# Masking the windowed attention of layer 1: additions on TensorE before the exponential, or multiplications on GpSimd and VectorE behind it

## The chip, the cores and the metric

The kernel is one program on one core of a Trainium2 chip. The metric is device time in microseconds (us) from launch to end; lower is better. Engines are named as in the profile: PE is TensorE (PEld its weight loads), DVE is VectorE, ACT is ScalarE, POOL is GpSimd, SP is SyncE.

## What is computed

Four sequences of 1024 tokens with 128 features pass through two layers. Each layer is an attention and a mixture of experts, each with a layer norm and a residual. Layer 1's attention has two halves in a row: a global causal one and a local one with a window of 32 keys. The change touches the local one alone. Cut to what matters:

```python
def local_gqa_attn(x, wq, wk, wv, wo):          # x: (1024, 128); H = 16 heads of 8, KVH = 4, WIN = 32
    q, k, v = split_heads(x @ wq, H), split_heads(x @ wk, KVH), split_heads(x @ wv, KVH)
    q, k = qk_norm(rope(q, BASE_L)), qk_norm(rope(k, BASE_L))
    k, v = repeat_kv(k), repeat_kv(v)
    diff = i[:, None] - i[None, :]
    mask = (diff >= 0) & (diff < WIN)
    scores = jnp.where(mask, einsum('bhqd,bhkd->bhqk', q, k) / sqrt(HD), -1e30)
    return merge_heads(einsum('bhqk,bhkd->bhqd', softmax(scores), v)) @ wo
```

The heads of q and k are normed, so the scores are small and the kernel takes no maximum off them. The softmax's sum comes from a column of ones beside the values (L1481), and DVE multiplies by its inverse at the end (L1814, L1818).

## The kernel before, in words

The program runs stage after stage: attention of layer 0, mixture of layer 0, `layer1_attention`, mixture of layer 1. `layer1_attention` has eight rounds (`ROUNDS`): rounds 0 to 3 are the global attention of the four sequences, rounds 4 to 7 the local one. A round has 32 steps (`STEPS`): four groups of four heads, by eight blocks of 128 keys. Each engine has one instruction queue, written out in the order of rounds and steps, and runs it strictly in that order; semaphores join the queues.

Two steps, 2k and 2k+1, make **pair k** of a round (pairs 0 to 15). In a local round PE does a pair as `local_pair` writes it: `score` of both steps (2 matmuls each, L1633, into the two score tiles `s_ps`), `mask_scores` of both (2 matmuls each, L1645: an identity times a tile of 0 and -1e30, added onto the scores), then `weigh` of the two steps of the pair before (4 or 8 matmuls each, L1664, probabilities by values), then `fill_banks`: transposes and projections that belong to the round before, this one or the next, into the two tiles `x_ps`. The table in `shared_uses` says which goes where.

A local step covers 128 keys by at most 160 queries for four heads, so its scores and probabilities are 128 partitions by 640 numbers (512 in a group's last key block, which is always an odd step). ACT takes the exponential (L1764) of both steps of a pair, then reads the `x_ps` tiles that are its own (L1730 to L1743). In step 18 to 22 of a round it also writes the high parts of the next round's heads (L1750), for which it waits until DVE has finished `scale_heads` (L1882) of step 17. The probabilities lie in three tiles `probsT` of 1024 queries' width, step s in tile s % 3, so that ACT waits for the `weigh` of three steps ago (L1762).

DVE and POOL make the next round's inputs meanwhile. DVE in a local round: `keep_output` (L1829) at steps 0, 4, 8 and so on, the reads of turned-back outputs (L1814, L1818) and of the output projection (L1824); `square_input`, `sum_input`, `scale_input` in steps 0, 1, 2 (L1838 to L1848); `rotate` in step 13 (L1854), `square_heads` in 14 (L1857), `sum_heads` in 15 (L1861 to L1864), `inverse_roots` in 16 (ten instructions from L1869 on), `scale_heads` in 17, `fill_slots` in 19 to 23 (L1893). In rounds 5 and 6 a layer norm of the round before comes on top in steps 22 to 29: statistics, its variance in step 26 (L69), normalisation in 27 and 28 (L74), the residual in 29 (L1907). In round 7 it is the norms for the next mixture. POOL in a local round: `input_root` in step 1 (L1490, waits for `sum_input`, and `scale_input` waits for it), `rotate` in 13 (L1496), `add_rotation` in 16 (L1502, waits for `sum_heads`), and from round 5 on `inverse_root` at step 25 (L90, waits for the variance that DVE works out in step 26). In the global rounds POOL also zeroes the diagonal block of every step's probabilities (`cut_diagonal`, L1509), and PE's `weigh` waits for that; in the local rounds it does not.

Of the kernel before, what the change touches and what calls it, by code (L numbers as in the profile page):

```python
# [7 lines left out]
BF16 = mybir.dt.bfloat16  # L8
# [7 lines left out]
P = 128  # L16
# [1309 lines left out]


def last_of_half(x, c):

    return max(n for n, kb in enumerate(order_of(x)) if any(a // HALF == c for a, _ in query_cols(x, kb)))  # L1330
# [56 lines left out]
def layer1_attention(nc, g):  # L1387


    with ExitStack() as ctx:  # L1390
# [36 lines left out]
        x_filled, x_read_act, x_read_dve = sem("x_filled"), sem("x_read_act"), sem("x_read_dve")  # L1427
        scored, exp_done, cut, pv_done, o_kept = (sem(n) for n in ("scored", "exp_done", "cut", "pv_done", "o_kept"))

        heads = QK // HD  # L1430
# [35 lines left out]
        with nc.Block() as block:  # L1466
# [8 lines left out]
            def _(pool):  # L1475
# [28 lines left out]
                def cut_diagonal(r, n):  # L1504
# [5 lines left out]
                                       compare_op=ALU.is_ge, fill=0.0, base=0, channel_multiplier=-1).then_inc(cut, 1)  # L1510

                for r in range(-1, ROUNDS + 1):
                    x = r + 1
                    for n in range(STEPS):
                        if 0 <= r < BATCH:
                            cut_diagonal(r, n)
                        if x in NORM_COUNT and n == 2:
                            inverse_root(pool, norm1, g.minus_half[:, 0:NB], NORM_COUNT[x])
# [23 lines left out]
            def _(pe):  # L1542
# [74 lines left out]
                def score(r, n, unit):  # L1617
# [12 lines left out]
                    for i in range(2):  # L1630
# [3 lines left out]
                                         start=True, stop=True, skip_group_check=True)  # L1634
                    if not is_local(r):
                        last.then_inc(scored, 1)

                def mask_scores(r, n):

                    kb, u = key_block(r, n), units_before(r, n)  # L1640
                    _, at_once, a, e = units_of(r, kb)[0]
                    for i in range(2):
                        out = s_ps[u % 2][:, i * HALF:i * HALF + at_once * (e - a)]
                        keeps = g.mask_window[:, 0:e - a].unsqueeze(1).to_broadcast([P, at_once, e - a])
                        last = pe.matmul(out.rearrange("p (j n) -> p j n", j=at_once), g.ident_bf[:], keeps, start=False,  # L1645
                                         stop=True, skip_group_check=True)
                    last.then_inc(scored, 1)

                def weigh(r, n, c):
# [3 lines left out]
                    a, e = cols[c]  # L1653
                    if is_local(r) or c:
                        pe.wait_ge(exp_done, UNITS_UP_TO[r, n])
                    else:
                        pe.wait_ge(cut, steps_up_to(r, n))
# [4 lines left out]
                    for place in range(GQ):  # L1662
                        col = a - kb * P if is_local(r) else a
                        last = pe.matmul(o_ps[place * SLOT:(place + 1) * SLOT, a:e],  # L1664
                                         values[r % 2][:, kb, head_at(s, place) // GQ, :],
                                         probsT[(r * STEPS + n) % 3][:, place // 2, place % 2, col:col + e - a], start=first,
                                         stop=True, skip_group_check=True)
# [25 lines left out]
                def local_pair(r, n):  # L1693

                    score(r, n, 0)
                    score(r, n + 1, 0)
                    mask_scores(r, n)
                    mask_scores(r, n + 1)
                    late_r, late_n = (r, n - 2) if n else (r - 1, STEPS - 2)
                    if is_local(late_r):  # L1700
                        weigh_all(late_r, late_n)
                        weigh_all(late_r, late_n + 1)
                    else:
                        weigh_last_of(late_r, late_n)
                    fill_banks(r, n)
                    fill_banks(r, n + 1)
# [15 lines left out]
            def _(act):  # L1722
# [30 lines left out]
                def exponents(r, n):  # L1753
                    step, kb = r * STEPS + n, key_block(r, n)
                    for unit, (j, at_once, a, e) in enumerate(units_of(r, kb)):
                        u = units_before(r, n) + unit
                        act.wait_ge(scored, u + 1)
                        if step >= 3 and unit == 0:

                            act.wait_ge(pv_done, step - 2)  # L1760
                        col = a - kb * P if is_local(r) else a
                        out = probsT[step % 3][:, :, j:j + at_once, col:col + e - a]  # L1762
                        src = s_ps[u % 2][:].rearrange("p (k n) -> p k n", k=2)[:, :, 0:at_once * (e - a)]
# [22 lines left out]
            def _(dve):  # L1786
# [124 lines left out]
                def norm_for_mixture():  # L1911
# [30 lines left out]
                    def scale_slots():  # L1942
                        dve.wait_ge(slot_rs_ready, 1)
                        for q in range(SB):
# [5 lines left out]
                            scale_slots, *(lambda q=q: normalize(range(2 * q, 2 * q + 2)) for q in range(4))]  # L1950

                for r in range(-1, ROUNDS + 1):
                    x = r + 1
# [5 lines left out]
                    if soft_parts:  # L1959
                        assert norm_chain.n == NORMS_TO_SECOND_RESIDUAL, norm_chain.n  # L1960
                    for n in range(STEPS):
                        for kept in outputs_kept_at(r, n):
                            keep_output(*kept)
# [549 lines left out]
def build(nc, aps, out):  # L2513
    g = Shared()
    g.inputs = aps
    with ExitStack() as ctx:
# [7 lines left out]
        g.mask_kq = sb("mask_kq", [P, P], BF16)  # L2524
        g.mask_window = sb("mask_window", [P, LOCAL_W], BF16)
        first_ctx = ctx.enter_context(ExitStack())
# [3 lines left out]
        with nc.Block() as block:  # L2530
# [13 lines left out]
            def _(dve):  # L2544
                dve.wait_ge(const_loaded, 4 * 16)
                dve.tensor_copy(g.ident_bf[:], g.ident[:])
                dve.tensor_copy(g.mask_kq[:], staged[0][:, 0:P])
                dve.tensor_copy(g.mask_window[:], staged[1][:])
        attention_layer0(nc, g)
# [25 lines left out]
```

## Time and profile before

| | |
|---|---|
| median of three runs | 2423.7 us (2423.76, 2423.70, 2411.78) |
| span of the profiled execution, first to last instruction | 2408.9 us |
| its own device time | not given apart from the span; the nearest run shown is 2411.78 us, 2.9 us above the span |
| busy share of the span | PE 91%, DVE 60%, ACT 51%, POOL 44% |
| `layer1_attention`'s local rounds | about 1956 to 2167 us of the span |

A busy share is the time in which the engine had an instruction running. The profile can list groups of instructions, stretches of time, waits with what ended them, and a timeline. In a timeline row the columns are start, length, engine, line, operation, output and inputs with their shapes, how many instructions were merged, and in brackets how long the engine had been idle and what released it.

### The profile page before, as it was taken

How to read it: one execution, taken by the hardware profiler on the slowest of the kernel's cores; microseconds unless marked ns; L12 is line 12 of the kernel's file. 1: busy time of each engine (PE TensorE's matmuls, PEld its weight loads, DVE VectorE, ACT ScalarE, POOL GpSimd, SP SyncE). 2: the span in 40 equal slices, each digit the busy share in tenths (PEclk: the TensorE clock that was granted, in tenths of full speed). 3: DMA queues.
4: the chain of work that ended last, by engine and by line, in shares of the span. 5: the costliest groups of instructions: out<-in, count | busy, mean ns of one | idle time of the engine just before them, and what ended most of it. 6: DMA issues, size and time to landing. Idle time of an engine off the chain costs nothing. (4 is left out here: it accounts for less than half of the span.)

```text
span 2408.9 us, 40334 instructions
## 1 busy us (share of the span) xinstructions
PE 2199.0 (91%) x15428; PEld 1390.3 (58%) x15428; DVE 1443.0 (60%) x3248; ACT 1224.4 (51%) x1788; POOL 1048.7 (44%) x980
## 2 busy tenths in 40 slices
PE   4999999999999999994999999969999998897787
PEld 2555565555555565543888888724434455555667
DVE  3677757776677757773556565555554555656533
ACT  2555545554465545541323333267786876664533
POOL 0777757776677757773223232433333321100001
PEclk9999999999999999997999999979999999999999
DMA  2000000000000000001200000000000000003001
GB/s 76 1 1 1 1 1 1 1 1 1 1 1 1 1 1 1 1 1 35 39 1 1 1 1 1 1 1 1 1 1 1 1 1 1 2 8 71 1 1 36
DMA packets 36323, 18.19 MB, mean 8 GB/s; under 512 B 16666, under 2 KB 33956, under 8 KB 36132
## 3 DMA queue, kind: packets, MB, share of 16 engines
q1 hardware_dynamic: 36132, 15.61, 2.6%
q8 instruction: 125, 2.05, 0.4%
q14 instruction: 66, 0.54, 0.1%
HBM read 13.50 MB, written 2.10 MB: 6 GB/s over the span
## 5 line engine op out<-in xcount | busy, mean ns | idle before, releaser
L311 POOL TENSOR_TENSOR a_first<-a_first,a_ring 128x512 f32<-128x512 f32 (+3 forms) x352 | 558.8, 1588 | 141.9 <-ACT a_ring L556 106.5
L1764 ACT ACTIVATE g_probsT<-g_s_ps 128x1024 f32<-128x1024 f32 (+2 forms) x448 | 368.9, 868 | 136.6 <-PE g_s_ps L1633 83.3
L556 ACT ACTIVATE a_ring<-a_st 128x768 f32<-128x768 f32 (+1 forms) x256 | 234.6, 916 | 262.8 <-PE a_st L463 262.8
L478 PE MATMUL a_o_ps<-a_ring,a_v 128*64 128x512 f32 (+3 forms) x1280 | 249.2, 485 | 3.4 <-POOL a_ring L293 2.4
L645 DVE RECIPROCAL a_row_inv<-a_row_inv 128x512 f32<-128x512 f32 x64 | 213.8, 3342 | 16.8 <-ACT a_row_inv L544 16.8
L1034 ACT ACTIVATE m_silu<-m_up,m_b 128x512 f32<-128x512 f32 x160 | 109.6, 688 | 221.9 <-PE m_up L966 219.1
L623 DVE TENSOR_REDUCE a_part_max<-a_mx 128x2 f32<-128x1024 f32 x128 | 156.5, 1222 | 102.4 <-PE a_mx L434 99.1
L1664 PE MATMUL g_o_ps<-g_probsT,g_values 128*32 128x512 f32 (+5 forms) x2688 | 206.7, 419 | 5.5 <-POOL g_probsT L1509 5.1
L1633 PE MATMUL g_s_ps<-g_qT,g_kT 64*128 64x512 f32 (+3 forms) x896 | 172.7, 433 | 28.0 <-ACT g_probsT L1764 22.4
L1509 POOL TENSOR_SCALAR_AFFINE_SELECT g_probsT<-g_probsT 128x512 f32<-128x512 f32 x128 | 88.0, 691 | 246.1 <-ACT g_probsT L1764 246.0
L630 DVE CUSTOM_DVE_ANT_0 a_masked<-a_mx,mask_wide,a_part_max 128x256 bf16<-128x256 f32 (+3 forms) x256 | 128.3, 548 | 91.1 <-PE a_mx L434 90.6
L887 POOL TENSOR_TENSOR m_acc<-m_acc,m_part 128x512 f32<-128x512 f32 x54 | 69.8, 1292 | 221.6 <-DVE m_part L1192 221.2
L630 DVE CUSTOM_DVE_ANT_0 a_masked<-a_mx,mask_wide 128x256 bf16<-128x256 f32 (+3 forms) x256 | 112.7, 487 | 82.6 <-PE a_mx L434 82.6
L1633 PEld LDWEIGHTS g_s_ps<-g_qT,g_kT 64*128 64x128 f32 x896 | 77.1, 187 | 140.9 <-ACT g_probsT L1764 98.4
L463 PE MATMUL a_st<-a_q_hi,a_k_hi 64*128 64x512 f32 (+3 forms) x768 | 150.7, 386 | 4.0 <-ACT a_shift L534 3.1
L434 PE MATMUL a_mx<-a_k_hi,a_q_hi 64*128 64x512 f32 (+3 forms) x768 | 141.0, 388 | 12.6 <-DVE a_largest L630 11.8
L980 PEld LDWEIGHTS m_down<-m_w,m_glu 128*128 128x128 f32 x1280 | 149.6, 192 | 3.5
L980 PE MATMUL m_down<-m_w,m_glu 128*128 128x128 f32 x1280 | 149.7, 275 | 0.0
L1180 DVE SCALAR_TENSOR_TENSOR m_glu<-m_up,m_b,m_silu 128x512 f32<-128x512 f32 x160 | 115.1, 745 | 45.5 <-ACT m_silu L1034 45.5
L463 PEld LDWEIGHTS a_st<-a_q_hi,a_k_hi 64*128 64x128 f32 x768 | 73.4, 185 | 113.8 <-ACT a_ring L556 79.1
L966 PE MATMUL m_up<-m_xT_hi,m_w_hi 128*128 128x512 f32 x320 | 134.1, 419 | 1.8 <-DVE m_xT_lo L1132 1.4
L463 PE MATMUL a_st<-a_q_hi,a_k_lo 64*128 64x512 f32 (+3 forms) x768 | 135.3, 344 | 0.0
(310 smaller groups left out, 4372.8 us busy)
## 6 DMA issues: line engine op xcount, KB each, us to landing
m_w<-in_L_ffn_rw SPq DMA_DIRECT2D x2, 1024.0 KB, 8.3
s_w<-in_L_ffn_w SPq DMA_DIRECT2D x1, 2048.0 KB, 9.0
s_w<-in_L_ffn_w SPq DMA_DIRECT2D x4, 512.0 KB, 10.2
out_x<-x SPq DMA_DIRECT2D x8, 256.0 KB, 2.3
m_w<-in_L_ffn_rw SPq DMA_DIRECT2D x2, 512.0 KB, 5.1
x<-in_L_attn_x SPq DMA_DIRECT2D x1, 512.0 KB, 4.5
a_outT<-in_L_attn_w_q SPq DMA_DIRECT2D x1, 512.0 KB, 5.4
a_outT<-in_L_attn_w_k SPq DMA_DIRECT2D x1, 512.0 KB, 6.0
```

The costliest lines, as they stand in the source:

```text
L311: pool.tensor_tensor(total[:, h, q:q + w], total[:, h, q:q + w], probs_of(n, u)[:, h, off:off + w], ALU.add).then_inc(added, 1)
L434: last = pe.matmul(mx_ps[:, h, off:off + w], q_hi[m % 2][rows_of(h), i * P:(i + 1) * P], k_hi[m % 2][rows_of(h), key:key + w], start=True, ...
L463: last = pe.matmul(out[:, h, off:off + w], a[rows_of(h)], r[rows_of(h)], start=i == 0, stop=i == len(todo) - 1)
L478: last = pe.matmul(o_ps[rows_of(h), first_q:first_q + w], v_half[n // 4 % 2][:, j, head:head + A_HD], probs_of(n, u)[:, h, off:off + w], s ...
L556: act.activation(probs_of(n, u)[:, :, 0:w], st_ps[u % 2][:, :, 0:w], ACT.Exp).then_inc(exp_done, 1)
L623: last = dve.tensor_reduce(part_max[:, i, :], mx_ps[:], AX.X, ALU.max)
L630: last = dve.tensor_tensor_reduce(masked[1 - part][:, h, 0:w], mx_ps[:, h, off:off + w], g.mask_wide[:, HALF - w:HALF], 1.0, so_far, ALU.a ...
L645: dve.reciprocal(row_inv[c][:], row_inv[c][:]).then_inc(inv_ready, 1)
L980: last = pe.matmul(down[u % 2][:, t * P:(t + 1) * P], glu[u % 2][h][:, t * P:(t + 1) * P], w3[:, e, h, :], start=h == 0 and t == 0, stop=h ...
L1633: last = pe.matmul(out, kT[r % 2][s // 2][rows, kb * P:(kb + 1) * P], qT[r % 2][rows, j:j + at_once, a:e], start=True, stop=True, skip_gro ...
L1664: last = pe.matmul(o_ps[place * SLOT:(place + 1) * SLOT, a:e], values[r % 2][:, kb, head_at(s, place) // GQ, :], probsT[(r * STEPS + n) % ...
L1764: act.activation(out, src.rearrange("p k (j n) -> p k j n", j=at_once), ACT.Exp, scale=float(HD) ** -0.5).then_inc(exp_done, 1)
```

## The change

The local rounds lose `mask_scores`. The tile of 0 and -1e30 (`mask_window`) becomes a tile of ones and zeros in bf16 (`mask_keep`), and `cut_window` multiplies each local step's probabilities by it, in place, after the exponential. POOL does it for even steps, at the head of the step in its queue, and counts `cut`. DVE does it for odd steps, at the head of the step in its queue, and counts `cut_odd`. PE's `weigh` waits for these counts where it waited for `exp_done`. `probs_place` gives the local rounds six places for probabilities: each of the three tiles is used in two halves (columns 0 to 159 and 256 to 415), so that ACT waits for the `weigh` of six steps ago.

```diff
+def probs_place(r, n):
+    step = r * STEPS + n
+    return step % 3, step % 6 // 3 * 256 if is_local(r) else 0
...
@@ gpsimd
+                def cut_window(r, n):
+                    w = units_of(r, key_block(r, n))[0][3] - key_block(r, n) * P
+                    buf, at = probs_place(r, n)
+                    probs = probsT[buf][:, :, :, at:at + w]
+                    keeps = g.mask_keep[:, 0:w].unsqueeze(1).unsqueeze(1).to_broadcast([P, 2, 2, w])
+                    pool.wait_ge(exp_done, UNITS_UP_TO[r, n])
+                    pool.tensor_tensor(probs, probs, keeps, ALU.mult).then_inc(cut, 1)
...
                         if 0 <= r < BATCH:
                             cut_diagonal(r, n)
+                        if BATCH <= r < ROUNDS and n % 2 == 0:
+                            cut_window(r, n)
                         if x in NORM_COUNT and n == 2:
...
@@ tensor
-                    if not is_local(r):
-                        last.then_inc(scored, 1)
-
-                def mask_scores(r, n):
-                    kb, u = key_block(r, n), units_before(r, n)
-                    _, at_once, a, e = units_of(r, kb)[0]
-                    for i in range(2):
-                        out = s_ps[u % 2][:, i * HALF:i * HALF + at_once * (e - a)]
-                        keeps = g.mask_window[:, 0:e - a].unsqueeze(1).to_broadcast([P, at_once, e - a])
-                        last = pe.matmul(out.rearrange("p (j n) -> p j n", j=at_once), g.ident_bf[:], keeps, start=False,
-                                         stop=True, skip_group_check=True)
                     last.then_inc(scored, 1)
...
-                    if is_local(r) or c:
+                    if is_local(r):
+                        done = steps_up_to(r, n) - BATCH * STEPS
+                        if n % 2:
+                            pe.wait_ge(cut_odd, done // 2)
+                        else:
+                            pe.wait_ge(cut, BATCH * STEPS + (done + 1) // 2)
+                    elif c:
                         pe.wait_ge(exp_done, UNITS_UP_TO[r, n])
...
                     score(r, n, 0)
                     score(r, n + 1, 0)
-                    mask_scores(r, n)
-                    mask_scores(r, n + 1)
...
@@ scalar
-                            act.wait_ge(pv_done, step - 2)
-                        col = a - kb * P if is_local(r) else a
-                        out = probsT[step % 3][:, :, j:j + at_once, col:col + e - a]
+                            act.wait_ge(pv_done, step - 5 if step >= BATCH * STEPS + 3 else step - 2)
+                        buf, at = probs_place(r, n)
+                        col = at + a - kb * P if is_local(r) else a
+                        out = probsT[buf][:, :, j:j + at_once, col:col + e - a]
...
@@ vector: the same cut_window, with dve and .then_inc(cut_odd, 1)
                     for n in range(STEPS):
+                        if BATCH <= r < ROUNDS and n % 2:
+                            cut_window(r, n)
                         for kept in outputs_kept_at(r, n):
                             keep_output(*kept)
...
@@ build
-                dve.tensor_copy(g.mask_window[:], staged[1][:])
+                dve.tensor_scalar(g.mask_keep[:], staged[1][:], 0.0, None, ALU.is_ge)
```

## Rows read from the trace of the kernel before

**Rows 1.** The page, part 1: busy time of the engines over the span

```profile
PE 2199.0 (91%) x15428; PEld 1390.3 (58%) x15428; DVE 1443.0 (60%) x3248; ACT 1224.4 (51%) x1788; POOL 1048.7 (44%) x980
```

**Rows 2.** Busy time in stretches: the local rounds, then three parts of them

```profile
core 0: us, PE busy (x) PEld busy (x) DVE busy (x) ACT busy (x) POOL busy (x), PEclk, DMA share, GB/s
1956.00:2167.00 211.00, 186.09 (x2114) 122.05 (x2112) 121.07 (x318) 133.52 (x236) 30.13 (x18) 0.97 0.01 3
...
1996.00:2009.00 13.00, 12.93 (x128) 7.93 (x128) 4.47 (x14) 10.39 (x20) 0.00 (x0) 0.80 0.01 1
2009.00:2035.00 26.00, 24.60 (x280) 16.89 (x280) 7.62 (x15) 19.56 (x36) 1.68 (x2) 1.00 0.01 2
2035.00:2051.00 16.00, 10.97 (x131) 7.36 (x129) 15.32 (x31) 5.32 (x10) 5.71 (x3) 1.00 0.00 1
```

**Rows 3.** Groups by line and shape, 1956 to 2167 us: exponentials and mask matmuls

```profile
L1764 ACT ACTIVATE g_probsT<-g_s_ps 128x640 f32<-128x640 f32 x112 | 78.1, 704 | 50.0 <-PE g_s_ps L1645 45.6 <-PE g_o_ps L1664 1.6
L1645 PE MATMUL g_s_ps<-mask_window,ident_bf 128*128 128x320 bf16 x224 | 42.8, 309 | 0.0
```

**Rows 4.** Timeline of PE: round 5's pairs 0, 3, 4, 7, 12, round 6's 0

```profile
2012.59 0.56 PE L1633 MATMUL g_s_ps<-g_qT,g_kT 64*128 64x320 f32 x4 [0.74 <-ACT g_qT L1732]
...
2021.96 0.53 PE L1633 MATMUL g_s_ps<-g_qT,g_kT 64*128 64x320 f32 x4
...
2024.73 0.56 PE L1633 MATMUL g_s_ps<-g_qT,g_kT 64*128 64x320 f32 x4
...
2034.17 0.53 PE L1633 MATMUL g_s_ps<-g_qT,g_kT 64*128 64x320 f32 x4
...
2055.17 0.85 PE L1633 MATMUL g_s_ps<-g_qT,g_kT 64*128 64x320 f32 x4
...
2067.86 0.56 PE L1633 MATMUL g_s_ps<-g_qT,g_kT 64*128 64x320 f32 x4 [0.74 <-ACT g_qT L1732]
```

**Rows 5.** Timelines of PE and of ACT: the rest of round 5's pair 4

```profile
2025.22 0.72 PE L1645 MATMUL g_s_ps<-mask_window,ident_bf 128*128 128x320 bf16 x4
2025.87 0.70 PE L1664 MATMUL g_o_ps<-g_probsT,g_values 128*32 128x160 f32 x16
2026.49 1.09 PE L1549 MATMUL g_x_ps<-ident,g_att 128*128 128x128 f32 x8
2027.52 0.56 PE L1633 MATMUL g_s_ps<-g_qT,g_kT 64*128 64x320 f32 x4
...
2025.70 1.48 ACT L1764 ACTIVATE g_probsT<-g_s_ps 128x640 f32<-128x640 f32 x2 [0.22 <-PE g_s_ps L1645]
2027.19 1.08 ACT L1738 ACTIVATE g_attT<-g_x_ps 128x512 f32<-128x512 f32 x2
```

**Rows 6.** Timeline, round 5's pairs 7 to 11: VectorE, GpSimd and PE's next scores

```profile
2034.93 0.82 DVE L1854 TENSOR_TENSOR g_part<-g_qk,g_cos 128x640 f32<-128x640 f32 x1 [1.43 <-ACT g_values L1743]
2034.97 1.92 POOL L1496 TENSOR_TENSOR g_part<-g_qk,g_sin 128x640 f32<-128x640 f32 x1 [15.46 <-ACT g_values L1743]
...
2035.67 1.90 DVE L1854 TENSOR_TENSOR g_part<-g_qk,g_sin 128x640 f32<-128x640 f32 x1
...
2036.85 1.85 POOL L1496 TENSOR_TENSOR g_part<-g_qk,g_cos 128x640 f32<-128x640 f32 x1
...
2038.04 2.00 DVE L1857 TENSOR_TENSOR g_turned<-g_qk 128x1280 f32<-128x1280 f32 x1
...
2048.28 1.48 DVE L1882 TENSOR_TENSOR g_turned<-g_turned,g_rs 128x1280 f32<-128x1280 f32 x1
...
2051.77 0.41 PE L1633 MATMUL g_s_ps<-g_qT,g_kT 64*128 64x320 f32 x2 [2.70 <-ACT g_probsT L1764]
```

**Rows 7.** GpSimd's multiplications and additions: a group, and one in a global round

```profile
L311 POOL TENSOR_TENSOR a_first<-a_first,a_ring 128x512 f32<-128x512 f32 x128 | 165.2, 1291 | 16.1 <-POOL a_ring L293 15.4 <-POOL a_first L311 0.5 <-ACT a_ring L556 0.2
...
1731.81 1.27 POOL L1496 TENSOR_TENSOR g_part<-g_qk,g_sin 128x640 f32<-128x640 f32 x1
```

**Rows 8.** Timeline, round 5's pairs 1 and 2: GpSimd's root, VectorE behind it

```profile
2017.86 1.65 POOL L1490 TENSOR_TENSOR g_rs_h<-g_ss_h,minus_half 128x8 f32<-128x8 f32 x1 [29.20 <-DVE g_ss_h L1844]
...
2019.54 1.23 DVE L1848 TENSOR_TENSOR normed<-hidden,g_rs_h 128x1024 f32<-128x1024 f32 x1 [1.00 <-POOL g_rs_h L1490]
```

**Rows 9.** Timeline, round 5's pairs 13 and 14: PE, and the norm's root

```profile
2061.09 0.91 PE L1633 MATMUL g_s_ps<-g_qT,g_kT 64*128 64x320 f32 x4
...
2062.22 1.65 POOL L90 TENSOR_TENSOR norm_rstd<-norm_var,minus_half 128x8 f32<-128x8 f32 x1 [17.78 <-DVE norm_var L69]
```

More of the change, by code:

```diff
@@ L1428, in layer1_attention @@
         scored, exp_done, cut, pv_done, o_kept = (sem(n) for n in ("scored", "exp_done", "cut", "pv_done", "o_kept"))
+        cut_odd = sem("cut_odd")
         heads = QK // HD
@@ L1662, in weigh @@
                     for place in range(GQ):
-                        col = a - kb * P if is_local(r) else a
+                        buf, at = probs_place(r, n)
+                        col = at + a - kb * P if is_local(r) else a
                         last = pe.matmul(o_ps[place * SLOT:(place + 1) * SLOT, a:e],
                                          values[r % 2][:, kb, head_at(s, place) // GQ, :],
-                                         probsT[(r * STEPS + n) % 3][:, place // 2, place % 2, col:col + e - a], start=first,
+                                         probsT[buf][:, place // 2, place % 2, col:col + e - a], start=first,
                                          stop=True, skip_group_check=True)
@@ L1758, in exponents @@
                         if step >= 3 and unit == 0:
-                            act.wait_ge(pv_done, step - 2)
-                        col = a - kb * P if is_local(r) else a
-                        out = probsT[step % 3][:, :, j:j + at_once, col:col + e - a]
+                            act.wait_ge(pv_done, step - 5 if step >= BATCH * STEPS + 3 else step - 2)
+                        buf, at = probs_place(r, n)
+                        col = at + a - kb * P if is_local(r) else a
+                        out = probsT[buf][:, :, j:j + at_once, col:col + e - a]
                         src = s_ps[u % 2][:].rearrange("p (k n) -> p k n", k=2)[:, :, 0:at_once * (e - a)]
@@ L1950, in norm_for_mixture, with cut_window @@
                             scale_slots, *(lambda q=q: normalize(range(2 * q, 2 * q + 2)) for q in range(4))]
+                def cut_window(r, n):
+                    w = units_of(r, key_block(r, n))[0][3] - key_block(r, n) * P
+                    buf, at = probs_place(r, n)
+                    probs = probsT[buf][:, :, :, at:at + w]
+                    keeps = g.mask_keep[:, 0:w].unsqueeze(1).unsqueeze(1).to_broadcast([P, 2, 2, w])
+                    dve.wait_ge(exp_done, UNITS_UP_TO[r, n])
+                    dve.tensor_tensor(probs, probs, keeps, ALU.mult).then_inc(cut_odd, 1)
                 for r in range(-1, ROUNDS + 1):
@@ L2524, in build @@
         g.mask_kq = sb("mask_kq", [P, P], BF16)
-        g.mask_window = sb("mask_window", [P, LOCAL_W], BF16)
+        g.mask_keep = sb("mask_keep", [P, LOCAL_W], BF16)
         first_ctx = ctx.enter_context(ExitStack())
```

## The prediction, made before the change was run

> **What bounds the kernel now.** I began with the page: PE is busy for 91% of the span [rows 1], so one would expect matmuls taken away to be time won. But the change lives in the local rounds alone, 211 us, so I read that stretch. There PE is busy for 186.1, ACT for 133.5, DVE for 121.1 and POOL for 30.1 us [rows 2]. These shares average over two regimes. From 2009 to 2035 us PE is busy for 24.6 of 26 us: PE sets the pace. From 2035 to 2051 DVE is busy for 15.3 of 16 us and PE for only 11.0: DVE's queue sets it [rows 2].
>
> I cut round 5 by the starts of its pairs [rows 4]: A, pairs 0 to 2, 9.37 us; B, pairs 3 to 6, 12.21; C, pairs 7 to 11, 21.00; D, pairs 12 to 15, 12.69; together 55.27. Rounds 4 and 6 repeat it within a microsecond, except that round 4 has no layer norm in D. Round 7 has no next round's heads to make.
>
> Pair 4 is the clean PE-bound one: scores at 2024.73, masks at 2025.22, `weigh` at 2025.87, fill at 2026.49, next pair at 2027.52. The masks take 0.65 of its 2.79 us. ACT works 1.48 + 1.08 us of them [rows 4, 5].
>
> **What goes.** 256 mask matmuls, of which the 224 wide ones are 42.8 us busy [rows 3]. On PE's path it is 0.65 us a pair, 41.6 us over 64 pairs if PE bounded all. It doesn't. In pairs 3 and 4 ACT then needs 1.45 + 1.08 = 2.53 us a pair, so 0.26 is won, not 0.65. In the projection pairs 5 and 6 PE's fill is longer, and 0.5 each is won. B: 2 x 0.26 + 2 x 0.5 = **1.6 us won a round**.
>
> **What comes.** 64 multiplications of 128x640 on POOL and 64 on DVE (48 of 640, 16 of 512). On DVE one costs 0.82, about 0.75 back to back, by L1854 [rows 6]. On POOL the same size, also with a broadcast operand, took 1.27 when undisturbed, and 512 dense elements took 1.29, so 640 would take at most 1.61 [rows 7]. The new one is dense like the second and broadcast like the first; I take 1.4. What the bf16 operand does no row shows; I put it at nothing. [...]
>
> **They shut each other out.** In rows 6 DVE's first product runs 2034.93 to 2035.75 and POOL's, begun at 2034.97, ends at 2036.89: 0.82 of waiting and 1.13 of work. DVE's second ends at 2037.57, 0.68 after that; POOL's second at 2038.70, 1.13 after that; DVE's L1857 at 2040.04, 1.34 after that. They take strict turns. So I charge a turn wherever a POOL cut meets a DVE instruction with two inputs in SBUF. The skill's page SBUF — State Buffer, section "Who interferes with whom", states it as an exclusive lock for the whole instruction, which speaks against giving the two halves of this mask to these two engines; the trace agrees. Were there no such turns, the sum below would be about +3 us instead of +21.
>
> **The order of the queues.** `weigh` of a step waited for ACT; now it waits for a cut standing in POOL's or DVE's queue behind all that these do for other rounds. Before, DVE could lag by more than a pair without PE noticing.
>
> A. POOL's cut 0 (1.4) blocks DVE's `square_input` for about 0.7, and cut 1 (0.75) stands before `sum_input`. POOL's root then ends at 2019.51 in the old times [rows 8], cut 2 comes after it (2020.9) and blocks `scale_input` (1.15, to 2022.05); then cut 3 (0.8), the read of a bank (0.6) and the second half of pair 2's fill (0.55): pair 3 at about 2024.0 + 1.4 instead of 2021.96, 3.5 late. Less 0.65 and some slack won in pairs 0 and 1: **+2.5**.
>
> C. DVE's chain from `rotate` to `scale_heads` runs 2034.93 to 2049.76, 14.8 us without a gap, and pair 11 waits for it through ACT: 2.70 us idle [rows 6]. Into it go cuts 15 and 17 (2 x 0.75), POOL's cut 14, which gets its turn after L1857 and before cut 15 (1.4), and POOL's cut 18 among `inverse_roots` (1.3 to 1.4): 4.2 to 4.3. PE stands meanwhile in pair 8 for cut 14, and in pair 9 some 8 us for cut 17, queued behind `inverse_roots`; that it then does pair 10 late adds little. **+4.4**.
>
> D. In rounds 5 and 6 the norm's root ends at 2063.87 [rows 9]. It stands in POOL's queue before cut 26, which so ends at 2065.3, while `weigh` of step 26 would be due at 2061.09 + 0.5: up to 3.7 late. Cuts 25, 27 and 29 lengthen DVE's queue beside the norm (4 x 0.75 in D). Less about 1 won: **+2.5**. In round 4 there is no norm: ACT-bound, **-1.9**.
>
> Round 7 has no chain C, but two roots (steps 3, 7) and the norm's at 25 before a cut: about +2, +1, +2.5; its other pairs win 3: **+2.5**.
>
> Free: two more waits on PE, the wider choice of places (ACT waited only 1.6 us for `weigh` in the wide group, [rows 3]), one constant made by another operation. No DMA moves, and SP's queue isn't touched.
>
> **Sum.** 3 x 2.5 - 3 x 1.6 + 3 x 4.4 - 1.9 + 2 x 2.5 + 2.5 = +21.5 us on the profiled span of 2408.9. The median of the runs is 14.8 above that span; I add the sum to the median: **2445 us**, +0.9%. Measurement of this kernel can tell about 0.5%, 12 us, from no change.
>
> **Rivals.**
> - *The order costs little.* POOL and DVE take turns less often, or the waits overlap more than by my hand count. The no-turns case, +3 us: 2427. For it: DVE has half of the stretch free. Against: the 15.3 of 16 us. Chance 0.25.
> - *PE's saving comes through.* DVE would have to have each odd cut done one pair later, at most some 3.3 us after the scores. Then half the pairs win 0.26 and half 0.6: 64 x 0.43 = 27 us, 2397. For it: 24.6 of 26 us PE-bound, POOL busy for only 30 of 211. Against: chain C. Chance 0.12. This is the case on the other side; it decides wherever DVE has under about 0.8 us of other work per pair, as in B.
> - *The clock falls.* After PE's first long wait the granted clock is 0.80 over 13 us [rows 2], partly the 1.2 GHz level; there PE is busy for 12.93 of 13. With waits of 5 and 8 us in C, and more in A and D, PE could come back at that level each time. If some 10 us of full-clock work a round at twice its time come in the open in part, 6 us a round: about +40, 2464. Chance 0.13.
> - That it doesn't do what it says I hold for unlikely: the cut products have their own semaphore, and nothing else reads uncut places.
>
> **How the numbers follow.** Main case +21 (chance 0.5; own range +10 to +33). Range 2414 to 2466: below it lies nearly all of the second rival, above it the tail of the third. A tenth of the main case lies within 12 us of no change, and the first rival all of it: same 0.25 + 0.05 = 0.30, slower 0.45 + 0.13 = 0.58, faster 0.12.
>
> **What would show it.** No L1645 rows. POOL rows of 1.3 to 1.5 us, longer when DVE is at a two-input product, and 128 more DVE and POOL rows. PE idle before L1664 with POOL and DVE as releasers, 20 us a round or more; in pair 9 one wait of about 8 us. Pairs 3 to 6 of a round in about 10.6 us; `rotate` to `scale_heads` in 19 us instead of 14.8. Wrong would be: local rounds shorter than 211 us; cuts on DVE that never wait for POOL; or a POOL cut above 2 us, which would make POOL the bound.

## The result, and the profile of the changed kernel

The changed kernel takes **2463.93 us** (median of four runs, 2462.47 to 2467.45), the kernel before 2419.75 (four runs, 2411.78 to 2423.76): a ratio of 1.0194, with an interval of 1.0165 to 1.0223. I had forecast 2445, slower. The direction is right and the time lies in the range, but the loss is 44.2 us where my sum said 21.5. The kernel before ran 54 times more beside the experiments, with medians of 2415.94, 2416.48 and 2415.98 us; against these the loss is 48 us.

The page, part 1, answers to [rows 1]:

```profile
PE 2193.7 (89%) x15172; PEld 1390.3 (57%) x15172; DVE 1536.0 (62%) x3312; ACT 1216.7 (49%) x1788; POOL 1151.6 (47%) x1044
```

256 matmuls are gone and PE is busy for only 5.3 us less. DVE has 93.0 us more, POOL 102.9 more.

The start of the local rounds wanders by some 15 us from one execution to the next, with the same code ahead of it, so I compare their length, from the first local score to the end of the last output projection, in the one profiled execution of each kernel. Where kernels have the same code in a section this length repeats well: section C of round 5 (pairs 7 to 11) takes 21.00 us in the kernel before and 21.01 and 21.02 in two kernels further down that leave it alone. Busy time in stretches, the kernel before (a stretch not shown above, with its last round):

```profile
1955.00:2171.40 216.40, 190.47 (x2144) 125.53 (x2144) 123.14 (x325) 135.40 (x239) 30.38 (x18) 0.97 0.01 3
...
2123.00:2171.40 48.40, 44.80 (x536) 29.46 (x536) 27.00 (x99) 26.54 (x40) 4.28 (x3) 1.00 0.04 10
```

The same for the changed kernel, then its round 5 in C and in D, and its round 7:

```profile
1952.20:2221.70 269.50, 186.30 (x1888) 124.06 (x1888) 215.36 (x389) 126.89 (x239) 133.41 (x82) 0.78 0.01 3
...
2044.59:2068.87 24.28, 14.57 (x142) 9.76 (x141) 23.20 (x41) 9.29 (x23) 13.65 (x9) 0.72 0.00 1
2068.87:2089.08 20.21, 13.33 (x124) 8.87 (x120) 16.07 (x39) 10.04 (x18) 9.20 (x6) 0.66 0.00 1
...
2160.00:2221.70 61.70, 43.76 (x472) 27.83 (x472) 49.84 (x114) 24.68 (x40) 28.74 (x19) 0.78 0.02 5
```

The whole loss is here: 269.5 - 216.4 = **53.1 us**, beside 51.8 between the two profiled spans (2460.7 and 2408.9). PE has 256 of 2144 matmuls fewer and is busy for nearly as long as before, with a granted clock of 0.78 where it was 0.97: partly the 1.2 GHz level. It is idle for 83.2 us instead of 25.9. DVE is busy for 80% of the stretch, before for 57%, and in C for 23.2 of 24.3 us. In C it sets the pace; elsewhere PE waits in turn for its cuts and for POOL's.

The waits of the local rounds (engine, what waited, who released it: us in total, times, longest) say how PE feels it:

```profile
PE g_o_ps L1678 <- DVE g_probsT L1972: 41.5, 28, 4.4
PE g_o_ps L1678 <- POOL g_probsT L1526: 38.6, 22, 4.4
```

80.1 of PE's 83.2 idle us stand before `weigh` (L1678), half of them put down to each engine's cuts. In the kernel before, PE's only wait there was this one:

```profile
PE g_o_ps L1664 <- ACT g_probsT L1764: 0.4, 1, 0.4
```

Groups of instructions by line and shape, and one tile (lowest, median and longest ns), in the same stretch:

```profile
L1972 DVE TENSOR_TENSOR g_probsT<-g_probsT,mask_keep 128x640 f32<-128x640 f32 x48 | 50.8, 1057 | 2.6 <-ACT g_probsT L1777 2.5
L1972 DVE TENSOR_TENSOR g_probsT<-g_probsT,mask_keep 128x512 f32<-128x512 f32 x16 | 21.4, 1337 | 8.1 <-ACT g_probsT L1777 8.1
L74 DVE TENSOR_SCALAR hidden<-hidden,norm_mean,norm_rstd 128x128 f32<-128x128 f32 x24 | 14.3, 655 | 2.9 <-POOL norm_rstd L90 2.9
...
L1526 POOL TENSOR_TENSOR g_probsT<-g_probsT,mask_keep x64: 1388/1407/2678, 1953.6 to 2210.5; 128x640 f32<-128x640 f32 x64
```

POOL's cut costs 1.41 us by its median, as taken (1.4). DVE's costs 1.06 and 1.34 by its means, and the smaller shape, a group's last key block, costs *more*: a mean that runs against the size is a sign that the instruction waits inside its own record. In this stretch 13 of the 16 smaller ones run beside a cut of POOL's and take 1.49 us on average, the other three 0.68. And an instruction with which the change has nothing to do, the norm's L74, takes 655 ns. Before it took 341 (and the integer `tensor_scalar` of `inverse_roots`, needed further down, 410):

```profile
L74 DVE TENSOR_SCALAR hidden<-hidden,norm_mean,norm_rstd 128x128 f32<-128x128 f32 x24 | 6.7, 341 | 3.6 <-POOL norm_rstd L90 3.6
...
L1869 DVE TENSOR_SCALAR g_rs<-g_ssq 128x160 int32<-128x160 int32 x3 | 1.2, 410 | 0.0
```

The timeline of the changed kernel's round 5, in A, C and D, answers to [rows 4, 6, 8, 9]:

```profile
2018.62 0.56 PE L1651 MATMUL g_s_ps<-g_qT,g_kT 64*128 64x320 f32 x4 [0.74 <-ACT g_qT L1744]
...
2024.50 1.65 POOL L1497 TENSOR_TENSOR g_rs_h<-g_ss_h,minus_half 128x8 f32<-128x8 f32 x1 [3.23 <-DVE g_ss_h L1857]
...
2026.12 3.73 POOL L1526 TENSOR_TENSOR g_probsT<-g_probsT,mask_keep 128x640 f32<-128x640 f32 x2
2026.18 2.41 DVE L1861 TENSOR_TENSOR normed<-hidden,g_rs_h 128x1024 f32<-128x1024 f32 x1 [1.21 <-POOL g_rs_h L1497]
...
2028.52 2.01 DVE L1972 TENSOR_TENSOR g_probsT<-g_probsT,mask_keep 128x640 f32<-128x640 f32 x1
...
2030.58 0.76 PE L1678 MATMUL g_o_ps<-g_probsT,g_values 128*32 128x128 f32 x16 [2.54 <-DVE g_probsT L1972]
...
2033.17 0.85 PE L1651 MATMUL g_s_ps<-g_qT,g_kT 64*128 64x320 f32 x4
...
2044.59 0.53 PE L1651 MATMUL g_s_ps<-g_qT,g_kT 64*128 64x320 f32 x4
...
2049.09 4.44 POOL L1526 TENSOR_TENSOR g_probsT<-g_probsT,mask_keep 128x640 f32<-128x640 f32 x2
...
2051.78 1.20 PE L1678 MATMUL g_o_ps<-g_probsT,g_values 128*32 128x160 f32 x16 [4.40 <-POOL g_probsT L1526]
...
2061.85 0.76 PE L1678 MATMUL g_o_ps<-g_probsT,g_values 128*32 128x160 f32 x8 [4.44 <-DVE g_probsT L1972]
...
2068.87 0.56 PE L1651 MATMUL g_s_ps<-g_qT,g_kT 64*128 64x320 f32 x4
...
2078.83 2.16 POOL L90 TENSOR_TENSOR norm_rstd<-norm_var,minus_half 128x8 f32<-128x8 f32 x1 [7.29 <-DVE norm_var L69]
...
2080.96 2.75 POOL L1526 TENSOR_TENSOR g_probsT<-g_probsT,mask_keep 128x640 f32<-128x640 f32 x2
2081.03 3.28 DVE L74 TENSOR_SCALAR hidden<-hidden,norm_mean,norm_rstd 128x128 f32<-128x128 f32 x4 [0.98 <-POOL norm_rstd L90]
2082.41 1.30 PE L1678 MATMUL g_o_ps<-g_probsT,g_values 128*32 128x160 f32 x24 [4.14 <-POOL g_probsT L1526]
...
2089.08 0.56 PE L1651 MATMUL g_s_ps<-g_qT,g_kT 64*128 64x320 f32 x4 [0.74 <-ACT g_qT L1744]
```

The starts of the scores cut the round as in the prediction (us):

| round 5 | A | B | C | D | sum |
|---|---|---|---|---|---|
| before | 9.37 | 12.21 | 21.00 | 12.69 | 55.27 |
| after | 14.55 | 11.42 | 24.28 | 20.21 | 70.46 |
| difference, measured | +5.2 | -0.8 | +3.3 | +7.5 | +15.2 |
| difference, forecast | +2.5 | -1.6 | +4.4 | +2.5 | +7.8 |

By rounds it is +8.8, +15.2, +15.7 and +13.3 us in rounds 4 to 7, where I had +3.4, +7.8, +7.8 and +2.5. So C is sized about right, B wins half of its gain, and what failed is A, D and round 7.

### The profile page after: what moved, and what is told of

Its sections match the earlier page's. It is cut to its first block and busy times, and to the rows that moved or that the text cites. A ratio compares the mean times of both kernels' runs of the same rounds, so it can differ in the third digit from the quotient of the medians.

```text
span 2460.7 us, 39950 instructions
## 1 busy us (share of the span) xinstructions
PE 2193.7 (89%) x15172; PEld 1390.3 (57%) x15172; DVE 1536.0 (62%) x3312; ACT 1216.7 (49%) x1788; POOL 1151.6 (47%) x1044
## 5 line engine op out<-in xcount | busy, mean ns | idle before, releaser
L1777 ACT ACTIVATE g_probsT<-g_s_ps 128x1024 f32<-128x1024 f32 (+2 forms) x448 | 362.7, 869 | 144.4 <-PE g_s_ps L1651 141.9
L1678 PE MATMUL g_o_ps<-g_probsT,g_values 128*32 128x512 f32 (+5 forms) x2688 | 222.2, 439 | 85.8 <-DVE g_probsT L1972 41.5
L1678 PEld LDWEIGHTS g_o_ps<-g_probsT,g_values 128*32 128x32 f32 x2688 | 68.1, 117 | 188.1 <-DVE g_probsT L1972 54.8
L434 PE MATMUL a_mx<-a_k_hi,a_q_hi 64*128 64x512 f32 (+3 forms) x768 | 141.1, 388 | 12.5 <-DVE a_largest L630 11.8
L1526 POOL TENSOR_TENSOR g_probsT<-g_probsT,mask_keep 128x640 f32<-128x640 f32 x64 | 101.9, 1598 | 86.7 <-ACT g_probsT L1777 86.7
```

Of the source, the lines that this page charges most:

```text
L434: last = pe.matmul(mx_ps[:, h, off:off + w], q_hi[m % 2][rows_of(h), i * P:(i + 1) * P], k_hi[m % 2][rows_of(h), key:key + w], start=True, ...
L1777: act.activation(out, src.rearrange("p k (j n) -> p k j n", j=at_once), ACT.Exp, scale=float(HD) ** -0.5).then_inc(exp_done, 1)
```

## The experiments

**Does it lie in the removal, the order or the work?** Three kernels take the change apart. The first is the changed kernel with no cut at all:

```diff
-                        if BATCH <= r < ROUNDS and n % 2 == 0:
-                            cut_window(r, n)
...
-                    if is_local(r):
...
+                    if is_local(r) or c:
                         pe.wait_ge(exp_done, UNITS_UP_TO[r, n])
```

> Leaves out the window's mask altogether (no masks on TensorE, no cuts): TensorE's weigh waits for the exponential alone, with the six places. It is the price of the removal by itself. By my prediction's sum the pairs bound by TensorE or ScalarE win 0.26 to 0.65 us each and the chain on VectorE stays: 15 to 27 us faster than before (ratio 0.989 to 0.994). If the removal itself were of no use, or harmful through the granted clock, it would be within 6 us of before.

Measured: 2397.57 us, 0.9923 of before (0.9895 to 0.9952), as expected.

The second keeps every cut, its place and its waits, but makes it 8 elements wide (on POOL and on DVE):

```diff
-                    probs = probsT[buf][:, :, :, at:at + w]
-                    keeps = g.mask_keep[:, 0:w].unsqueeze(1).unsqueeze(1).to_broadcast([P, 2, 2, w])
+                    probs = probsT[buf][:, 0, 0, at:at + 8]
+                    keeps = g.mask_keep[:, 0:8]
```

> Every cut stays where it stands in the two queues, with its waits and counts, but multiplies 8 columns of one head instead of all (so most of the mask is left out). Theory 1, the order of the queues: TensorE still waits in pairs 2, 8, 9, 14 for what stands ahead of the cuts, so most of the loss stays: slower than before by 10 to 25 us. Theory 2, the load and the turns at SBUF: with products of about 0.2 us the loss is gone, and the time is that of the kernel without cuts plus 5 us at most.

Measured: 2407.24 us, 0.9961 (0.9938 to 0.9984): between the two theories, 9.7 us above the kernel without cuts. A small cut takes 0.2 us on POOL and 0.16 on DVE, by their medians.

The third does nearly all the multiplying, on columns of the tiles that nobody uses in the local rounds, and no other engine waits for it (`weigh` waits for `exp_done`, as in the first). It has 62 products an engine instead of 64, since the first two pairs of round 4 have none, and each product also waits for the one three before it on its own engine, which is not shown:

```diff
-                    probs = probsT[buf][:, :, :, at:at + w]
+                    probs = probsT[0][:, :, :, 512:512 + w]
...
-                    pool.tensor_tensor(probs, probs, keeps, ALU.mult).then_inc(cut, 1)
+                    pool.tensor_tensor(probs, probsT[2][:, :, :, 512:512 + w], keeps, ALU.mult).then_inc(cut, 1)
...
-                    probs = probsT[buf][:, :, :, at:at + w]
+                    probs = probsT[1][:, :, :, 512:512 + w]
...
-                    dve.tensor_tensor(probs, probs, keeps, ALU.mult).then_inc(cut_odd, 1)
+                    dve.tensor_tensor(probs, probsT[2][:, :, :, 512:512 + w], keeps, ALU.mult).then_inc(cut_odd, 1)
```

> The full products stay in both queues at the same places, but read and write unused columns (512 on) of the probability tiles, and TensorE's weigh waits for the exponential alone (the mask is left out of the result). Theory 2, load and turns: near the changed kernel, at least 30 us slower than before. Theory 1, order: only VectorE's chain of pairs 7 to 11 is longer, by 4 us a round, against what the removal wins: within 12 us of before.

Measured: 2449.68 us, 1.0139 (1.0111 to 1.0167): theory 2.

Their local rounds, in this order, each row from its own kernel's stretches:

```profile
1965.00:2159.70 194.70, 157.83 (x1888) 111.89 (x1888) 122.37 (x325) 125.51 (x239) 30.37 (x18) 0.89 0.01 4
```

```profile
1967.50:2171.20 203.70, 167.47 (x1888) 115.86 (x1888) 129.98 (x389) 125.55 (x239) 50.09 (x82) 0.87 0.01 3
```

```profile
1957.20:2208.60 251.40, 175.05 (x1888) 121.65 (x1888) 217.65 (x387) 126.13 (x239) 127.00 (x80) 0.80 0.01 3
```

From 216.4 of before: the removal (with the six places) gives 21.7 us back; the order of the queues costs 203.7 - 194.7 = 9.0; the work costs 251.4 - 194.7 = **56.7**, though no other engine waits for its result. The medians of whole executions say 18.4, 9.7 and 52.1. With both one would expect 260.4; the changed kernel has 269.5, 9 us more. That remainder is a balance: by rounds it is +7.4, +5.5, +2.7 and -6.7 us, for in round 7 the work alone (65.7 us) is slower than the changed kernel (61.7). In round 5's D the work alone adds 0.6 us and the order alone 1.3 to the 12.5 of the first kernel, both together 7.8: there the late cuts and PE's wait for them feed each other.

**Whose work?** The same load with only POOL's 62 products (DVE's call taken out), then with only DVE's (POOL's taken out):

```diff
@@ vector, for POOL's alone
-                        if BATCH <= r < ROUNDS and n % 2:
-                            cut_window(r, n)
@@ gpsimd, for DVE's alone
-                        if BATCH <= r < ROUNDS and n % 2 == 0:
-                            cut_window(r, n)
```

> Of the load experiment only GpSimd's 62 products stay, on unused columns; VectorE has none and nobody waits for a cut (the mask is left out). If turns at SBUF carry the loss: 12 to 25 us above the kernel without cuts, with two-input products of VectorE drawn out to 1.4 us more. If VectorE's own products carry it: within 5 us of the kernel without cuts.

> Of the load experiment only VectorE's 62 products stay (the mask is left out). If VectorE's own time carries the loss: 30 to 50 us above the kernel without cuts, since 62 products of 0.8 us are 50 us in its queue. If turns carry it: 5 to 15 us, the products in its bound stretches alone (2 or 3 a round, 0.75 each, in three rounds).

Measured: 2428.51 us, 1.0043 (1.0025 to 1.0060), with POOL's, more than I had expected; 2407.29 us, 0.9971 (0.9958 to 0.9984), with DVE's. POOL's first:

```profile
1960.60:2188.50 227.90, 169.80 (x1888) 120.23 (x1888) 153.54 (x325) 126.02 (x239) 123.23 (x80) 0.82 0.01 3
```

```profile
1956.20:2167.60 211.40, 167.29 (x1888) 117.14 (x1888) 164.72 (x387) 125.88 (x239) 32.10 (x18) 0.84 0.02 3
```

In the first of them DVE has exactly the 325 instructions of the kernel without cuts, and is busy for 153.5 us instead of 122.4. The local rounds are 33.2 us longer, about those 31. DVE's own 62 products add 42.3 us to its queue and only 16.7 to the rounds. So a product on POOL, which had been busy for only 30 of 216 us, costs twice what it costs on DVE itself (by the medians of whole executions 30.9 us against 9.7). It isn't that POOL's roots come late behind the products: DVE's waits for POOL's results add up to 8.8 us with and without them. The timeline of POOL's load in round 7 shows how a product costs so much:

```profile
2151.12 7.94 POOL L1529 TENSOR_TENSOR g_probsT<-g_probsT,mask_keep 128x640 f32<-128x640 f32 x5
2151.18 3.43 DVE L1955 SCALAR_TENSOR_TENSOR normed<-normed,hidden 128x128 f32<-128x128 f32 x4 [0.53 <-POOL hidden L1557]
...
2154.65 3.15 DVE L1933 TENSOR_SCALAR hidden<-x,hidden 128x128 f32<-128x128 f32 x4
...
2160.65 3.42 PE L1614 MATMUL g_x_ps<-g_w_o,g_attT 128*128 128x128 f32 x16 [4.94 <-DVE g_att L1828]
```

POOL had stood in a root that waits for DVE. Five cuts had piled up behind it, and they now run back to back. Beside each of them one small DVE instruction waits for about its length, and at most one more passes before the next: four of L1955 in 3.43 us, four of L1933 in 3.15, and PE stands 4.94 us for what DVE does next. And L1933 is a `tensor_scalar`: a form that I had not counted among those that wait.

**Reads or writes?** POOL's products of the third kernel become memsets of about the same length, which read nothing:

```diff
-                    pool.tensor_tensor(probs, probsT[2][:, :, :, 512:512 + w], keeps, ALU.mult).then_inc(cut, 1)
+                    pool.memset(probsT[0][:, :, :, 512:888], 0.0).then_inc(cut, 1)
```

> The load experiment with GpSimd's products replaced by memsets of 1504 elements (about 1.4 us, the same length and places), which read nothing from SBUF; VectorE's products stay (the mask is left out). If GpSimd's reading is what shuts VectorE out: the time of the run with VectorE's products alone, within 5 us. If any work of GpSimd does: the time of the load experiment.

Measured: 2425.66 us, 1.0042 (1.0027 to 1.0057), local rounds of 227.8 us, 16.4 more than with DVE's products alone: the expectation missed. Groups by line show why:

```profile
L1529 POOL MEMSET g_probsT<- 128x1504 f32 x62 | 83.9, 1353 | 64.0 <-ACT g_probsT L1774 61.3 <-POOL g_probsT L1529 0.4
L1973 DVE TENSOR_TENSOR g_probsT<-g_probsT,mask_keep 128x640 f32<-128x640 f32 x46 | 38.0, 825 | 5.5 <-ACT g_probsT L1774 5.4
L74 DVE TENSOR_SCALAR hidden<-hidden,norm_mean,norm_rstd 128x128 f32<-128x128 f32 x24 | 15.0, 1117 | 2.9 <-POOL norm_rstd L90 2.9
L1973 DVE TENSOR_TENSOR g_probsT<-g_probsT,mask_keep 128x512 f32<-128x512 f32 x16 | 10.9, 684 | 5.7 <-ACT g_probsT L1774 5.7
L1879 DVE TENSOR_SCALAR g_rs<-g_ssq 128x160 int32<-128x160 int32 x3 | 5.0, 1683 | 0.0
...
L1955 DVE SCALAR_TENSOR_TENSOR normed<-normed,hidden 128x128 f32<-128x128 f32 x4 | 1.1, 348 | 0.1
```

Here is the same group of products with no load on POOL:

```profile
L1971 DVE TENSOR_TENSOR g_probsT<-g_probsT,mask_keep 128x640 f32<-128x640 f32 x46 | 37.6, 818 | 5.7 <-ACT g_probsT L1772 5.6
L1971 DVE TENSOR_TENSOR g_probsT<-g_probsT,mask_keep 128x512 f32<-128x512 f32 x16 | 11.0, 686 | 6.1 <-ACT g_probsT L1772 6.1
```

Beside POOL's writes a DVE product runs undisturbed (825 against 818 ns, 684 against 686), and L1955 with two inputs too (348 ns, where POOL's products made it 916). The `tensor_scalar` instructions wait all the more: L74 takes 1117 ns instead of 342. So beside POOL's reads DVE's instructions with two inputs in SBUF wait, and beside POOL's writes `tensor_scalar` does; a product does both. Not every form waits. Beside POOL's products (the run with these alone) DVE's copies out of PSUM and its reductions stay within 2 ns of the kernel without cuts (686 and 1474 ns):

```profile
L1839 DVE COPY g_outT<-g_o_ps 128x512 f32<-128x512 f32 x34 | 23.3, 686 | 39.6 <-PE g_o_ps L1675 39.6
...
L1871 DVE TENSOR_REDUCE g_ssq<-g_turned 128x160 f32<-128x1280 f32 x3 | 4.4, 1476 | 0.0
```

Of the 34 copies 19 run at the same time as one of POOL's products, and so do all three of these reductions.

**Would one engine alone do better?** All 128 cuts on DVE, then all on POOL; `weigh` waits for that engine's count alone:

```diff
@@ vector, for all on DVE (POOL's call taken out)
-                        if BATCH <= r < ROUNDS and n % 2:
+                        if BATCH <= r < ROUNDS:
                             cut_window(r, n)
@@ gpsimd, for all on POOL (DVE's call taken out)
-                        if BATCH <= r < ROUNDS and n % 2 == 0:
+                        if BATCH <= r < ROUNDS:
                             cut_window(r, n)
```

> All 128 cuts on VectorE, each at the head of its step, none on GpSimd; the mask is whole. Turns theory (VectorE's loss is mostly waiting for GpSimd's products, 44 us in the changed kernel): 128 products are about 98 us in VectorE's queue, but without turns, so faster than the changed kernel by 15 to 35 us, 2430 to 2450 us, products at 0.82 and 0.68 us in every round. Own-load theory (VectorE's products themselves are the loss): slower than the changed kernel, above 2470 us.

> All 128 cuts on GpSimd, none on VectorE; the mask is whole. Turns theory: twice as many GpSimd products of 1.4 us, 180 us and more in its queue; VectorE's other work in the local rounds is drawn out by about 60 us (31 with 62 products), and the roots stand behind more cuts: slower than the changed kernel, 2470 to 2500 us. If it were the sum of both engines' work that counts, it would be within 10 us of the changed kernel.

Measured: 2459.42 us, 1.0188 (1.0160 to 1.0216), and 2475.20, 1.0245 (1.0219 to 1.0270). All on DVE, then all on POOL:

```profile
1953.40:2210.60 257.20, 185.65 (x1888) 120.48 (x1888) 218.12 (x453) 127.06 (x239) 34.40 (x18) 0.79 0.01 3
```

```profile
1959.70:2235.40 275.70, 193.50 (x1888) 124.59 (x1888) 183.29 (x325) 126.98 (x239) 213.84 (x146) 0.77 0.01 3
```

With twice the cuts and no turns DVE is busy for 218.1 us; with half of them and the turns it was 215.4. The help of POOL is worth nothing to DVE. Taking the turns away gains 12.3 us in the profiled execution, but only 4.5 by the medians, which their intervals can't tell from nothing. Neither of the two times that I had named came (2430 to 2450, or above 2470): the queue on DVE is as full as before. With all cuts on POOL, DVE's own work is drawn out by 60.2 us (183.3 against the 123.1 of before).

**Is it the clock?** The granted clock fell as in my third rival, and its time, 2464, is the measured one. To test it, PE gets idle matmuls before `weigh` in pairs 2, 8, 9 and 14, where it would stand anyway; first in all local rounds, then in rounds 4 to 6:

```diff
+                SPINS = {2: 20, 8: 20, 9: 22, 14: 20}
...
+                            for _ in range(SPINS[n // 2]):
+                                pe.matmul(x_ps[k % 2][:, 0:480].rearrange("p (j n) -> p j n", j=3), g.ident_bf[:], keeps, start=True, stop=True, skip_group_check=True)
```

> The changed kernel, and TensorE runs 20 to 22 idle matmuls of 480 columns (about 0.2 us each at full clock, results unused) before weigh in pairs 2, 8, 9 and 14 of each local round, where it waits longest. Theory 3, the granted clock that falls after long waits carries a large part of the loss: granted clock of the local rounds above 0.9 instead of 0.78 and 15 to 25 us faster than the changed kernel. If the clock's loss lies in time that TensorE would wait anyway: within 6 us of the changed kernel; if the idle matmuls outlast the waits: slower.

> As the run with idle matmuls, but only in rounds 4 to 6, since in round 7 they stood where TensorE had no long wait. If the granted clock carries some of the loss: 5 to 10 us faster than the changed kernel (2.6 us a round was seen in rounds 5 and 6). If it carries none: within 3 us of it.

Measured: 2473.01 us, 1.0235 (1.0209 to 1.0262), and 2464.37, 1.0209 (1.0181 to 1.0237). The stretch of each:

```profile
1959.50:2233.20 273.70, 229.73 (x2196) 137.27 (x2196) 216.36 (x389) 126.02 (x239) 131.56 (x82) 0.91 0.01 3
```

```profile
1954.50:2220.90 266.40, 219.88 (x2134) 133.00 (x2134) 217.47 (x389) 126.25 (x239) 132.43 (x82) 0.89 0.01 3
```

The clock rises from 0.78 to 0.91 and 0.89, so the low clock follows from PE's waits. The first wins 2.5 and 2.7 us in rounds 5 and 6 and loses 8.9 in round 7. The second wins as much in rounds 5 and 6, loses 1.4 us in round 7, where its code is that of the changed kernel, has 3.1 us shorter local rounds in all, and the same median as the changed kernel, where I had named 5 to 10 us less if the clock carried some of the loss. Its idle matmuls:

```profile
L1716 PE MATMUL g_x_ps<-mask_keep,ident_bf 128*128 128x480 bf16 x246 | 51.9, 367 | 5.4 <-DVE g_att L1844 3.7 <-DVE hidden L1850 1.7
```

Without them PE is busy for 219.9 - 51.9 = 168.0 us, 18.3 less than in the changed kernel, yet only 3.1 us of that come through. Either it lies in time in which PE would wait for DVE and POOL anyway, or the idle matmuls, which themselves stand 5.4 us for a bank, take back part of what the clock gives; these runs cannot tell the two apart.

**A version that keeps only what wins.** By the table B is the one section that gains. The next kernel takes the masks on PE everywhere, as before, except in steps 6 to 13 of each local round, where POOL cuts the even and DVE the odd steps:

```diff
+CUT_STEPS = range(6, 14)
+is_cut = lambda n: n in CUT_STEPS
...
+                    if not is_cut(n):
+                        mask_scores(r, n)
+                        mask_scores(r, n + 1)
```

> Cuts only in steps 6 to 13 of each local round (pairs 3 to 6, where VectorE is idle), the mask matmuls everywhere else. Theory: these pairs win about 2 us a round and lose nothing elsewhere: 5 to 9 us faster than before (ratio 0.996 to 0.998). The rival, that cuts cost wherever they stand: no faster than before.

Measured: 2418.16 us, 1.0016 (1.0001 to 1.0030), no faster than before: the expectation missed. Rounds 4 to 6 won 2.6, 1.5 and 1.0 us; round 7, which has DVE work of its own there, lost 6.5. So the last kernel moves round 7's cuts to steps 14 to 23 and gives all of them, even and odd, to DVE:

```diff
+CUT_STEPS = {r: range(14, 24) if r == ROUNDS - 1 else range(6, 14) for r in range(BATCH, ROUNDS)}
...
+                        if BATCH <= r < ROUNDS and is_cut(r, n):
+                            cut_window(r, n)
```

> The mask stays on TensorE except in pairs 3 to 6 of rounds 4 to 6 and pairs 7 to 11 of round 7, where VectorE is mostly idle and cuts all steps alone. No GpSimd product, so no turns. Expected: 2 us won in each of rounds 4 to 6 and 2 to 4 us in round 7, 8 to 10 us faster than before (ratio 0.9955 to 0.997). If cuts on VectorE cost as much as masks on TensorE even there: within 4 us of before.

Measured: **2409.92 us** (twelve runs) beside 2415.98 of before, 0.9971 (0.9954 to 0.9988).

```profile
1957.60:2169.00 211.40, 183.18 (x2076) 120.96 (x2076) 147.62 (x360) 127.60 (x239) 30.39 (x18) 0.95 0.01 3
```

Its 34 cuts give 5.0 us of local rounds, 1.0, 2.1, 1.3 and 0.6 by rounds, and in round 5 B takes 10.35 us instead of 12.21. It is 6 us faster than the kernel before, where I had expected 8 to 10.

## Why the prediction was right and wrong

**Right.** The loss sits in the local rounds; POOL's cut costs 1.40 us (1.41); the two engines take turns; DVE's queue and not PE's saving decides. In C `rotate` to `scale_heads` takes 18.4 us, from 2045.35 to 2063.79, where I had 19; PE waits for cut 14 in pair 8 (4.40 us), as told. B wins, 0.8 instead of 1.6.

**The step that failed** is "They shut each other out": "So I charge a turn wherever a POOL cut meets a DVE instruction with two inputs in SBUF." I charged 0.7 + 1.15 us in A and 1.4 + 1.35 in C, 4.6 a round, 14 us in rounds 4 to 6, and nothing in B, D and round 7. I set the case without turns 18.5 us below my sum (+3 and +21.5), though the turns that I charged make only 14 of that; the other 4.5 have no term. Measured, POOL's products cost 33.2 us alone and 6.8 more beside DVE's: **40 us** where nobody waits for them, and at most 49 if the whole remainder of 9.1 is theirs too, in place of 14 to 18.5. How much of these us is PE at the lower clock that comes with its waits stays open. On DVE itself some **43 us** can be counted. Its cuts take 50.8 + 21.4 = 72.2 us where 48 x 0.818 + 16 x 0.686 = 50.2 would be undisturbed: 22.0. Its other work takes 215.4 - 72.2 = 143.2 us against the 122.4 of the kernel without cuts: 20.8. Three things were missing from the term; how the missing us divide among them was not measured:

- *The form.* I counted only instructions with two inputs. The norm's `tensor_scalar` L74 goes from 341 to 655 ns in the changed kernel, 24 times (7.6 us), and 3.28 us for four of them stand in D. This is what the Trainium skill's page SBUF — State Buffer, section "Who interferes with whom", states beside the rule that I used: a two-input operation contends with GpSimd instructions that read, not with those that only write, while `tensor_scalar` can enter a mode that takes both pairs of ports, and then contends with GpSimd altogether. The trace agrees with both halves: 825 and 1117 ns beside a memset.
- *Every cut counts, not the ones drawn on the path.* DVE's own cuts meet POOL's in B, D and round 7. POOL has 64 cuts, and I had priced 12 turns.
- *They bunch.* POOL's cuts wait behind a root or for ACT, then run back to back, each holding one small DVE instruction for a whole cut: in A the two cuts at 2026.12 draw out `scale_input` from 1.23 [rows 8] to 2.41 us, and then DVE's cut 3 from 0.82 to 2.01. I let cut 2 through there but not the one behind it, and so had pair 3 3.5 us late, less 1 won. It is 5.2 late.

**D** was a second miss, +7.5 us for +2.5. The mechanism stands, a cut behind the norm's root: the root runs at 2078.83 for 2.16 us, cut 26 comes behind it and PE waits 4.14. But I priced only the root's 3.7 us. The variance for which it waits comes late as well, since DVE's cuts and turns stand before it (POOL idle for 7.29 us), and the four L74 behind it take turns with cuts 26 and 28. Work alone (0.6) and order alone (1.3) are both small; only the two together make 7.8.

**Round 7** (+13.3 us for +2.5): DVE goes from 27.0 us busy to 49.8, of which the 16 cuts are some 12.6 undisturbed. I gave it two roots and a norm for POOL and no turns at all.

**The case without turns comes out about right, from wrong parts, which is luck.** I had +3 for it. If the parts simply add up, which no run shows, it is -21.7 for the removal, +9.0 for the order and +16.7 for DVE's own products: +4.0. The removal I had at some 15 us (1.6 a round in B, 1.9 in round 4's D, 3 in round 7, and about 1 a round each netted off in A and D); most of the difference is in round 7, which wins 8.3. The order and DVE's products were too low by about as much. So the turns make the miss, as far as the parts add up. (A slip beside it: 2 x 0.26 + 2 x 0.5 is 1.5, not 1.6, for B.)

**The rivals.** "PE's saving comes through" is out: even without any cut only 22 of 42 us come through. "The clock falls": the granted clock fell, to 0.78, and its number is the measured one, but lifting the clock to 0.89 gives 3 us back and not the 18.5 by which that rival lay above the main case. That a rival's number fits is no evidence for its mechanism. It isn't wholly excluded either, since the clock didn't come back to 0.97 and the idle matmuls may have cost something. The prediction's own test, "one wait of about 8 us" in pair 9, showed 4.44: part of the delay had been spent in pair 8, which took 9.62 us (2046.82 to 2056.44), so that pair 9 began later.

In sum, of local length: -21.7 the removal, +9.0 the order, +56.7 the work (16.7 by DVE's products alone, 33.2 by POOL's alone, 6.8 more together), +9.1 where work and order meet: 53.1. D of rounds 5 and 6 has 5.8 and 5.9 us of the last term; what lies against it elsewhere was not taken apart.

## What to carry to other kernels

Work given to an idle GpSimd is not free for a busy VectorE: charge every GpSimd instruction that reads and writes SBUF with up to its whole length on VectorE's queue, wherever VectorE has a `tensor_scalar` on SBUF or an instruction with two SBUF inputs beside it (copies out of PSUM and reductions kept their times here), and look for places where GpSimd waits first and then runs its backlog in one piece. When TensorE sets the pace only in some stretches, take work off it only there, and give it to the engine that is really free there: 34 of 128 cuts, all on VectorE, were a gain, where all 128 on two engines were a loss of 1.9%.

## What was not expected of the hardware

A `tensor_scalar` on VectorE waits for a whole GpSimd product: four of 0.34 us took 3.28, beside two products. It waits for a GpSimd memset as well: L1879 took 1683 ns beside memsets and 410 in the kernel before, while products of two tiles beside the same memsets kept their time (825 against 818 ns). And 62 GpSimd products for which no other engine waits made the local rounds 33.2 us longer, the same number on VectorE itself 16.7.
